# A wait on GpSimd behind each four gathers of tile 0's expert rows, at the end of both expert mixtures

## What is computed

```python
x = x + 0.5 * moe(layernorm(x))          # mixture 1
x = x + attention0(layernorm(x))         # scan over time, 8 heads
x = x + 0.5 * moe(layernorm(x))          # mixture 2
x = x + 0.5 * ternary_mlp(layernorm(x))
x = x + linear_attention(layernorm(x))
x = x + 0.5 * ternary_mlp(layernorm(x))

def moe(x):                              # N = 4096 tokens
    shared = gelu(x @ Wfc_s + bfc_s) @ Wproj_s + bproj_s
    gate = top 2 of softmax(x @ Wr), renormalised, of 8 experts
    routed = sum over e of (gelu(x @ Wfc[e] + bfc[e]) @ Wproj[e] + bproj[e]) * gate[:, e]
    return shared + routed
```

## Time and profile before

| | |
|---|---|
| median of 3 runs | 1119.49 us (1116.87 to 1121.55) |
| the profiled execution's own time | 1125.22 us |
| its span, first to last instruction | 1123.5 us |
| busy in it: TensorE, VectorE, GpSimd, ScalarE | 999.3, 824.7, 639.0, 636.0 us |
| mean granted TensorE clock | 0.964 of full speed |
| gathers of result rows (L678) | 80 into `got`, 48 into `wr` |
| tile 0's first fetch in mixture 1, in mixture 2 | 240.6 us, 829.3 us |

### The profile page before, as it was taken

The page is one execution under the profiler, slowest core; times in us unless marked ns, Lnnn a source line. Parts: engine busy times, 40 slices in busy tenths (PEclk is TensorE's granted clock), DMA queues, the critical chain, the costliest instruction groups (busy, mean ns, idle before and its releaser), DMA issues.

```text
span 1123.5 us, 16233 instructions
## 1 busy us (share of the span) xinstructions
PE 999.3 (89%) x4744; PEld 700.8 (62%) x4744; DVE 824.7 (73%) x2327; ACT 636.0 (57%) x1265; POOL 639.0 (57%) x751
## 2 busy tenths in 40 slices
PE   6788989997989999999996997999895688999996
PEld 5335777774656777677674554777772456666663
DVE  7776787656877887878786685776654589998762
ACT  2435667764556666666663334777653446666633
POOL 5005556544998988987664005556443777775440
PEclk9899999998999999999996998999997889999999
DMA  8577667750000000000002005677740100110000
GB/s 266 187 250 281 217 213 246 241 168 26 18 10 15 15 13 15 15 11 1 2 1 66 10 1 169 224 233 240 234 152 15 33 24 20 29 29 10 11 10 29
DMA packets 63495, 105.26 MB, mean 94 GB/s; under 512 B 7888, under 2 KB 42192, under 8 KB 63376
## 3 DMA queue, kind: packets, MB, share of 16 engines
q1 hardware_dynamic: 54320, 85.60, 23.1%
q0 software_dynamic: 9088, 18.63, 6.0%
HBM read 79.29 MB, written 26.87 MB: 94 GB/s over the span
## 4 chain that ended last, share of the span: by engine, by line
PE 50%; POOL 19%; DVE 15%; issue 9%; ACT 3%; another core or an unknown queue 1%; DMA 1%; ACTq 0%; POOLq 0%; SPq 0%; DVEq 0%
PE bank L208 5%; POOL wr L678 3%; POOL head_rstd L1379 3%; PE bank L453 3%; PE bank L455 3%; PE bank L474 3%; PE bank L457 3%; PE bank L472 3%; PE bank L473 3%; PE bank L456 3%; PE bank L1193 2%; PE bank L466 2%; PE bank L1159 2%; PE bank L1153 2%; PE bank L1199 2%
## 5 line engine op out<-in xcount | busy, mean ns | idle before, releaser
L622 POOL DMA_INDIRECT spare_all<-xs,list_row x156 | 158.8, 1018 | 235.2 <-DVE list_row L786 108.2
L858 DVE TENSOR_TENSOR hid_lo<-hid,hid_hi 128x512 fp32r<-128x512 f32 (+1 forms) x184 | 111.7, 610 | 69.7 <-ACT hid L559 36.9
L559 ACT ACTIVATE hid<-bank,b_up_of 128x512 f32<-128x512 f32 (+1 forms) x184 | 113.0, 624 | 7.0 <-PE bank L457 2.3
L558 ACT ACTIVATE hid_hi<-bank,b_up_of 128x512 fp32r<-128x512 f32 (+1 forms) x138 | 86.8, 629 | 52.5 <-PE bank L457 34.8
L1272 ACT ACTIVATE gate_b<-bank,head_rstd 128x128 f32<-128x128 f32 x256 | 72.9, 368 | 72.6 <-POOL head_rstd L1379 71.0
L678 POOL DMA_INDIRECT got<-ys,y_slots x80 | 84.0, 1050 | 42.1 <-issue 41.8
L208 PEld LDWEIGHTS bank<-ident,spare_all 128*128 128x128 f32 x476 | 60.4, 149 | 68.5 <-issue 58.2
L559 ACT ACTIVATE hid<-bank,cols_sb 128x512 f32<-128x512 f32 x64 | 43.9, 687 | 96.0 <-PE bank L453 76.2
L208 PE MATMUL bank<-ident,spare_all 128*128 128x128 f32 x476 | 77.8, 287 | 21.1 <-DVE spare_all L401 14.8
L455 PE MATMUL bank<-xh,wr 128*128 128x512 f32 (+1 forms) x184 | 77.4, 421 | 16.3 <-DVE xl L850 6.9
L1379 POOL TENSOR_TENSOR head_rstd<-head_var,neg_half 128x4 f32<-128x4 f32 x64 | 78.3, 1223 | 5.3
(11 more groups left out here) (325 smaller groups left out, 2677.3 us busy)
## 6 DMA issues: line engine op xcount, KB each, us to landing
wr<-wq SPq DMA_DIRECT2D x92, 512.0 KB
wq<-wr SPq DMA_DIRECT2D x16, 512.0 KB, 5.7
ys<-spare_all SPq DMA_DIRECT2D x32, 256.0 KB
got<-in_w_mlp SPq DMA_DIRECT2D x8, 512.0 KB, 5.3
xs<-spare_all SPq DMA_DIRECT2D x16, 256.0 KB, 2.3
spare_all<-xs,list_row POOLq DMA_INDIRECT x156
out_x<-X SPq DMA_DIRECT2D x8, 256.0 KB, 2.3
ys<-in_x SPq DMA_DIRECT2D x1, 1920.0 KB
```

The costliest lines, as they stand in the source:

```text
L559: nc.scalar.activation(hid[:, n % HC, 0:w], bank[up_bank(n)][:, 0:w], ACT.Gelu_apprx_tanh, bias=bias).then_inc(s["gelu_done"], 1)
L622: g.indirect_dma_start(out=xin[:, j % XIN, b], out_offset=None, in_=xs, in_offset=bass.IndirectOffsetOnAxis(ap=list_row[:, n:n + 1], axis=0))\
L858: v.tensor_tensor(hid_lo[:, q, 0:w], hid[:, n % HC, 0:w], hid_hi[:, q, 0:w].bitcast(F32), ALU.subtract).then_inc(s["lo_done"], 1)
```

## The change

Behind parts 0 to 3 of tile 0, and again behind parts 4 to 7, GpSimd waits until the gathers issued so far have landed. Both mixtures call the function, so there are four such waits in an execution.

```diff
@@ -662,6 +662,8 @@
                     pool.wait_ge(*s.at("down_done", LISTS_END))
                 for n in range(half * TB, half * TB + TB):
                     moe_fetch(pool, s, i, n, ring)
+                if i == 0:
+                    pool.wait_ge(*s.at("fetched", 16 * TB * (half + 1), 0))
 
         def all_stored(eng, s):
             for m in range(YOUT):
```

## The result

The changed kernel takes 1128.89 us (median of six runs, 1127.30 to 1135.71) against 1119.33 us of the kernel before on the same chip (six runs, 1116.87 to 1122.37). The ratio is 1.0092 with a 95% interval from 1.0058 to 1.0126: it is slower by 9.6 us, where 2.1 us were forecast. The profiled execution took 1130.13 us with a span of 1128.4 us, only 4.9 us more than the one of before, which was itself 5.7 us above the median of its three runs. So the two profiles show half of the loss, and half of the study is about that gap. The measured median also lies just inside the upper end of the predicted range (1129 us), which was there for the rival "slower" and not for the forecast.

What follows compares the result with a forecast made beforehand. No engine bounds the whole; at the mixtures' ends TensorE was late, leaving GpSimd slack. 0.7 - 0.6 + 2.0 (clock) = +2.1 us on the 1119.5 us median gave 1121.6 us, range 1114 to 1129.

Steps and rivals of the forecast that it cites:

- the rival "slower": Ends of both mixtures: TensorE isn't held up outside the profile, so GpSimd's root delay counts in full, +11.4 us; chance 0.2.
- The waits themselves: GpSimd, tile 0: each landing takes 2.45 us; part 4 starts 1.2 us later and the root 5.7 us later.
- the reads behind the second wait: GpSimd's four store-count reads before tile 1's gathers, no longer made ahead: 2.5 us, plus 0.74 us to the gather.
- The slack: End of mixture 1: GpSimd's chain to the normalized tile has 5.1 us to spare; net +0.7 us, mixture 2 -0.6 us.
- The release that "nothing in the trace shows": ScalarE's last GELU in mixture 1 starts at 257.78, though TensorE had issued the products it needs by 253.85.
- What the waits give: Pauses between gather groups end TensorE's hold-up; in mixture 1 ScalarE's last GELU starts by 255.9 instead of 257.78.
- a stall: Ends of mixtures: a long unbroken gather run holds up TensorE's signals or work until 2.15 to 2.37 us after it.
- The clock: TensorE idles just before the next stage, which starts at half clock: 1.5 us in mixture 1, 0.5 in mixture 2.
- What is behind the root: Tile 1's second and tile 2's first four gathers start 5.7 us later: priced 0, at most 2 us in all.
- the other reading: Mixture 2's 4.98 us GELU delay could be TensorE's own lateness, not a held signal; the sum is the same.

Runs made afterwards that it cites:

- e13: The kernel before, unchanged, measured and traced on chip 5; its two measurements there gave ratios 0.9986 and 0.9993 against itself.

## Why the prediction was wrong

**The waits themselves.** Right. In the four traces of the change, the landing was 2.5 to 2.6 us for the second wait, and for the first 3.1 to 3.4 us in mixture 1 and 2.7 to 2.8 us in mixture 2 (2.45 forecast); the reads behind the second wait 2.9 us; the root 5.6 to 6.1 us later (5.7 forecast). The Trainium skill (DMA: Bandwidth & Descriptors, section "Anatomy of one DMA") would make such a landing 2.15 us, as an estimate; the landings in these traces, 2.5 to 3.4 us, are all above that.

**The slack.** This is the step that failed: "The chain through GpSimd has 5.1 us of slack there: TensorE is late, not GpSimd." It was read from one execution on one chip. In the traces of the kernel before on chips 2 and 5, and at the untouched site on chip 3, TensorE is ready 2 to 4 us before the normalized tile comes, and the root has no slack. What isn't shown is that the same happened in the measurement itself, on chip 1: the one trace of before counted to it has the slack, and the pair of traces doesn't explain the measured loss (below). The release that "nothing in the trace shows" should have been a warning that the lateness isn't a property of the program. I had it as the rival "slower", priced 2 x 5.7 = +11.4 us and given 0.2, and that price is what chips 3 and 5 measure. Its reason was off: recording alone doesn't hold TensorE up, since 15 recorded executions on three chips show nothing of it.

**What the waits give.** Right where there is a stall: with pauses behind the fourth and the eighth gather the GELUs are released at once, in both mixtures on chip 1 and in mixture 2 on chip 4. It gains nothing, because GpSimd's root is late by then. Which of the two pauses does it isn't known, since the kernels with one wait alone ran only on chips that hold nothing up.

**The clock.** Forecast 1.5 and 0.5 us. In the pair of chip 1, from the transpose to a later instruction of ScalarE (some 15 us behind it in mixture 1, 100 us in mixture 2), the changed kernel takes 2.2 and 1.6 us longer, 3.8 us where 2.0 were forecast. The windows of the changed kernel show TensorE's granted clock there, against 1.00 in the earlier trace rows:

```profile
267.00:270.00 3.00, 2.36 (x9) 1.99 (x10) 2.14 (x4) 1.07 (x2) 2.39 (x3) 0.50 0.16 44
270.00:273.00 3.00, 3.00 (x8) 2.33 (x8) 2.12 (x7) 1.18 (x2) 2.08 (x4) 0.50 0.18 49
273.00:276.00 3.00, 3.00 (x9) 1.98 (x8) 1.39 (x2) 1.58 (x3) 2.39 (x3) 0.57 0.20 64
```

It stays at half for the first nine products and more. But where TensorE isn't held up, the kernel before has that half clock too behind mixture 1, as it idles there as well. In its trace on chip 5 (e13):

```profile
257.00:260.00 3.00, 2.54 (x7) 2.07 (x7) 2.75 (x8) 0.69 (x1) 2.09 (x4) 0.50 0.20 49
260.00:263.00 3.00, 3.00 (x9) 2.20 (x9) 0.70 (x2) 1.45 (x3) 2.39 (x3) 0.55 0.18 46
```

So on those chips the clock costs nothing more in mixture 1: the same stretch behind the transpose takes as long with the change as without. In mixture 2 it is 106.1 to 108.1 us before and 107.9 to 108.8 us after, some 1.5 us in the mean.

**What is behind the root.** Tile 1's later fetch was priced at 0. In the change that holds, as nothing waits for it at that place. It holds only because the root is just as late: with the root on time, 10 us of delay of tile 1 cost 0.5%, nearly all of it in mixture 1.

**Half of the loss missing in the two profiles.** The traced execution of before was held up: from root to transpose it took 8.7 us in mixture 1 and 10.0 us in mixture 2, in place of 3.7. From the pair of traces the change costs 4.8 + 2.0 us at the two sites (ScalarE's instructions ahead of and behind each site, one by one). But 1.45 and 0.94 us of that are only the start of the first gather, which came that much later against the work ahead of it. It stands ahead of both waits, and it moves as much between traces where nothing was changed: against a fixed GELU of ScalarE it varies by 1.7 us over all traces in mixture 1 and by 1.3 us in mixture 2. What is left belongs to the change, in the prediction's own terms 1.1 - 0.6 us at the transposes and 3.8 us of clock, some 4.3 us or 0.4%. That is below the measured interval (0.58 to 1.26%). So the traced pair doesn't explain the 9.6 us of chip 1, and the cause of the rest stays open. If the untraced executions there are held up less than the traced one, it is nearer to the 11 us of the other chips; no run shows whether they are. On chip 4 the waits in mixture 2 alone cost 0.2%, less than the 0.5 to 0.8% expected of a chip that holds nothing up, which fits a held up one.

The Trainium skill (Perfetto Trace Analysis, section "Tensor Engine Instruction") was the other reading, a late end of the product itself, as ends in a profile are estimates. The chips show that the lateness doesn't belong to the program: the GELU that waits 8.51 us on chip 4 starts within 0.1 us of the modelled end of its product on chips 2, 3 and 5. Whether the product or its signal is late on chips 1 and 4 isn't shown by any run.

## What to carry to other kernels

Slack that a trace shows ahead of a release that no instruction explains is not slack to spend: take a second trace, on another chip if one can, before a wait is put in its place. When two traces are compared, check first that they agree ahead of the change: here 2.4 us of their difference were there before the first wait. A wait on an engine's list costs its own length and whatever cheap work the sequencer had done ahead of its turn; here four reads of 0.63 us made a landing of 2.5 us into a gap of 5.8. Of two waiting consumers behind one queue (the root, and tile 1's rows), an order that serves one better can cost as much at the other.

## What the runs showed of the hardware that was not expected

**On two of five chips what TensorE releases comes late while GpSimd gathers.** In each of the five traces of chips 1 and 4, at 5 to 10 places besides the ends of the mixtures, an idle ScalarE starts a GELU or a cast more than 1 us (up to 3.9 us) behind the latest modelled end of TensorE's work that it waits for, all of them among the expert lists, where GpSimd gathers. At the ends of the mixtures it is up to 8.6 us. In the 15 traces of chips 2, 3 and 5, with the same programs, no such start is more than 0.12 us late. That the gathers are the cause is argued from where it happens and from the pauses that end it, and not shown.

**The granted clock gives one kernel two lengths on one chip.** The kernel before was traced twice on chip 5 in one set of measurements, with spans of 1095.0 and 1103.3 us. Five of these 8.3 us lie between 600 and 632 us, a sparse stretch ahead of mixture 2. The longer execution is 6.0 us behind by 616 us, so the windows are set for the same products, first of the shorter execution, then of the longer:

```profile
616.00:620.00 4.00, 3.63 (x34) 3.54 (x34) 1.12 (x4) 1.65 (x3) 1.02 (x1) 1.00 0.24 67
```

```profile
624.00:628.00 4.00, 4.00 (x21) 4.00 (x21) 0.19 (x1) 1.87 (x2) 0.00 (x0) 0.50 0.22 66
```

The products that the shorter execution runs between 616.7 and 621.7 us, nearly all at full clock, the longer runs at half clock between 622.7 and 630.7 us, and 3.0 us are lost there. Over all traces the stretch takes one of three lengths, some 2.5 us apart (34.0 to 34.4, 36.8 to 37.0 and 39.1 to 39.3 us between two fixed instructions), with and without the change. That is half of the 10 us over which the executions of one kernel spread, and it makes a difference of a few microseconds between two single profiles unreadable until both are lined up instruction by instruction.
